# A Mamba, cross-attention and FFN layer on one core: output rows placed by indirect DMAs, norms by pairs, ups in plain fp32

## The chip, the core and the metric

The kernel runs on one core of a Trainium2 chip. The metric is the device time of one execution in microseconds, from the first to the last instruction of the program and what the runtime puts around it. Weights are laid out for the kernel on the host ahead of the launch, and the result is reshaped on the host after it; neither is in the time.

## The reference

The input x is 512 tokens (2 sequences of 256) by 512 features, float32. Three blocks follow each other, each on a layer norm of x, each with its result added to x:

```python
x = x + attn(layernorm(x))              # Mamba-2 block, 128 heads of 64
x = x + matmul(fake_quant(layernorm(x)), fake_quant(ctx))    # 8-bit levels, per sequence
x = x + ffn(layernorm(x))

def ffn(x):                              # 16 heads of 32 features
    t = x[:, perm].reshape(tokens, 16, 32)
    t = gelu(einsum('bhd,hdm->bhm', t, up))       # 32 -> 128, exact gelu
    t = einsum('bhm,hmd->bhd', t, down)           # 128 -> 32
    return t.reshape(tokens, 512)[:, argsort(perm)]

def fake_quant(x, s, z):
    return (clip(round(x / s + z), 0, 255) - z) * s
```

The attention block projects x to 8 groups of 1024 channels with gates and states, takes the RMS norm of each group, and multiplies by an output weight; its last steps are the only ones that the change touches. `perm` is a permutation of the 512 features.

## The kernel before

Everything up to the last group of the attention block (some 740 us of the 809) is a software pipeline over 8 groups of 8 tiles, and the change leaves it alone but for a memset and a small copy. What follows runs once, in straight code, with the order of each engine's instructions written out by hand and semaphores between the engines. Tokens lie in four tiles of 128 (`t`), features in four blocks of 128 (`k`). An fp32 matmul of full precision is made of two or three passes on values split into a high and a low part of type float32r (`h_hi`, `h_lo`), the high part by ScalarE, the low part by VectorE or GpSimd; a matmul on plain float32 takes its operands as they are stored.

1. Attention's end. TensorE multiplies the last three tiles of the group (`out_tile`, 12 matmuls each) and, ahead of the very last one, sums the squares over channels (`last_token_sums`, L1437). VectorE turns the sums to means (L1108), GpSimd raises them to the power -1/2 (L581), and VectorE adds the four token tiles to the residual `res` (L1112). Before that VectorE builds eight 0/1 matrices, `take` and `put` (L999, L1001), which stand for the permutation.
2. Norm for the quantised product. Per pair of token tiles: statistics, power on GpSimd (L640), scale and offset (L1225 to L1227), ScalarE scales (L860), VectorE rounds in two steps (L1232, L1233).
3. Quantised product. TensorE sums the columns of the quantised context `q2` (L1525, one output row), runs 18 matmuls whose result nobody reads (`keep_busy`, WARM_A, L1518), multiplies `negrow` by the column sums with one row of weights (L1533), turns the rounded tiles (L1541), multiplies them (L1549), sums them (L1555), and runs 20 more unread matmuls (WARM_B).
4. Norm for the FFN. VectorE adds the product to `res` (L1268) and normalises all four tiles (L1237); TensorE turns them so that features lie in the partitions (L1566); ScalarE and VectorE split (L876, L1287).
5. FFN. 32 matmuls with `take` permute the features (L1574), and the result is split again (L882, L1291). For each k there are four heads in two pairs: `up_pair` in three passes (L1587), gelu on ScalarE (L885), `down_product` in plain fp32 (L1595).
6. Putting back. VectorE splits the down products (L1296, L1297), 32 matmuls with `put` restore the feature order and turn the result back to tokens by features (`put_back`, L1603), VectorE adds it to `res` (L1301), and SyncE stores four tiles (L502).

## Time and profile before

| what | us |
|---|---|
| median of 3 runs | 809.83 (809.65 to 810.01) |
| the profiled execution's own time | 810.87 |
| its span, first to last instruction | 809.0 |
| mean granted TensorE clock | 0.991 of full |

| engine | busy, share of the span |
|---|---|
| TensorE | 787.9 us, 97% |
| VectorE | 712.9 us, 88% |
| GpSimd | 589.1 us, 73% |
| ScalarE | 548.3 us, 68% |

Busy shares are an average over stages. In the last 68 us, of which this document speaks, the engines hand work to each other, and what matters is which of them ends each wait. Times in a timeline are counted from the start of the span. A matmul in plain fp32 leaves two records in the trace for each one in the program, so that x8 stands for four of them.

### The profile page before, as it was taken

What the parts mean: (1) busy time and instruction counts of PE and PEld (TensorE: products, weight loads), DVE (VectorE), ACT (ScalarE), POOL (GpSimd) and SP (SyncE); (2) the same over time, 40 slices, a digit from 0 to 9 for tenths busy, and PEclk for the clock granted to TensorE, in tenths of its full rate; (3) what the DMA queues carried; (4) which work ended last, traced back from release to release, by engine and by line L of the source; (5) the groups of instructions that cost most, each with busy time, mean ns of one, the idle gap of its engine ahead of it and who ended that gap; (6) DMA issues with size and microseconds to landing.
All of it is one profiled execution on the core that took longest, in us unless ns stands there. A gap on an engine that the chain in (4) does not pass through costs nothing.

```text
span 809.0 us, 14438 instructions
## 1 busy us (share of the span) xinstructions
PE 787.9 (97%) x4244; PEld 615.8 (76%) x4244; DVE 712.9 (88%) x919; ACT 548.3 (68%) x1138; POOL 589.1 (73%) x484
## 2 busy tenths in 40 slices
PE   7989999999999999999999999999999999999987
PEld 6767777777877778777887778877778777777454
DVE  6989999998998989998999989998999989998753
ACT  4777776776676776776667776766667677886242
POOL 5469777887778877797778877788778877785100
PEclk9999999999999999999999999999999999999899
DMA  7453344433443345533454244543444544521001
GB/s 234 154 201 125 125 157 170 157 117 132 169 165 118 119 156 169 169 130 104 168 169 146 101 154 155 169 155 107 144 165 156 166 166 149 184 78 40 1 1 53
DMA packets 44051, 111.14 MB, mean 137 GB/s; under 512 B 5748, under 2 KB 6644, under 8 KB 44020
## 3 DMA queue, kind: packets, MB, share of 16 engines
q1 hardware_dynamic: 44020, 110.76, 40.1%
q8 instruction: 15, 0.25, 0.1%
q14 instruction: 16, 0.13, 0.0%
HBM read 109.30 MB, written 1.44 MB: 137 GB/s over the span
## 4 chain that ended last, share of the span: by engine, by line
PE 93%; DVE 4%; ACT 1%; issue 1%; DMA 1%; POOL 0%; ACTq 0%; SPq 0%; DVEq 0%
PE ps_in L1309 17%; PE ps_in L1311 15%; PE ps_in L1310 15%; PE ps_y L1421 8%; PE ps_o L1309 7%; PE ps_o L1311 7%; PE ps_o L1310 7%; PE ps_y L1424 3%; PE ps_t L1383 3%; PE ps_t L1395 1%; PE ps_o L1603 1%; PE ps_t L1433 1%; PE ps_o L1549 1%; PE ps_o L1587 1%; DVE hid L1010 1%
## 5 line engine op out<-in xcount | busy, mean ns | idle before, releaser
L539 POOL TENSOR_TENSOR w_lo<-raw,w_hi 128x512 fp32r<-128x512 f32 x144 | 233.4, 1642 | 102.9 <-ACT w_hi L647 101.6
L1309 PE MATMUL ps_in<-h_hi,w_hi 128*128 128x512 f32 x560 | 226.3, 404 | 2.8 <-DVE gate L1029 2.8
L1311 PE MATMUL ps_in<-h_hi,w_lo 128*128 128x512 f32 x560 | 219.6, 392 | 0.0
L1310 PE MATMUL ps_in<-h_lo,w_hi 128*128 128x512 f32 x560 | 218.4, 390 | 0.0
L702 ACT ACTIVATE e<-e,nag 128x256 f32<-128x256 f32 (+1 forms) x512 | 183.6, 444 | 2.9 <-DVE nag L1080 2.9
L1010 DVE SCALAR_TENSOR_TENSOR hid<-ps_in,curc,hid 128x510 f32<-128x510 f32 x183 | 136.0, 743 | 4.4
L1309 PEld LDWEIGHTS ps_in<-h_hi,w_hi 128*128 128x128 f32 x560 | 105.1, 188 | 33.2 <-issue 10.5
L1311 PEld LDWEIGHTS ps_in<-h_hi,w_lo 128*128 128x128 f32 x560 | 105.4, 188 | 23.3
L570 POOL TENSOR_TENSOR e<-e,gm 128x512 f32<-128x512 f32 x64 | 100.5, 1570 | 30.8 <-DVE gm L1054 26.8
L1310 PEld LDWEIGHTS ps_in<-h_lo,w_hi 128*128 128x128 f32 x560 | 105.5, 188 | 20.4
L667 ACT ACTIVATE hid<-ps_in,curc 128x512 f32<-128x512 f32 x61 | 47.4, 777 | 102.9 <-PE ps_in L1311 102.7
L1066 DVE TENSOR_TENSOR e<-e,gm 128x1024 f32<-128x1024 f32 x64 | 107.8, 1684 | 2.1 <-DVE curc L1071 1.0
L1309 PE MATMUL ps_o<-wo_hi,z_hi 128*128 128x512 f32 x256 | 101.5, 396 | 0.0
L1311 PE MATMUL ps_o<-wo_hi,z_lo 128*128 128x512 f32 x256 | 99.9, 390 | 0.0
L1310 PE MATMUL ps_o<-wo_lo,z_hi 128*128 128x512 f32 x256 | 99.7, 389 | 0.0
L549 POOL TENSOR_TENSOR wo_lo<-rawo,wo_hi 128x512 fp32r<-128x512 f32 x64 | 85.6, 1337 | 5.3 <-ACT wo_hi L655 5.3
L716 ACT ACTIVATE z_hi<-z,curs 128x512 fp32r<-128x512 f32 x64 | 46.2, 722 | 61.0 <-DVE z L1097 61.0
L1421 PE MATMUL ps_y<-e,hdt 128*64 128x256 f32 x512 | 80.7, 393 | 4.2 <-issue 2.3
L559 POOL TENSOR_SCALAR_AFFINE_SELECT e<-e 128x512 f32<-128x512 f32 x128 | 80.2, 651 | 5.6 <-DMA e<-acs_rows 5.6
L647 ACT ACTIVATE w_hi<-raw 128x512 fp32r<-128x512 f32 x144 | 82.0, 622 | 0.4 <-DMA raw<-in_w_in 0.4
L1097 DVE TENSOR_TENSOR z<-z,gate 128x512 f32<-128x512 f32 x64 | 78.6, 1229 | 2.2
L1037 DVE TENSOR_TENSOR hdt<-ps_t,dtg 128x512 f32<-128x512 f32 x64 | 44.1, 688 | 37.0 <-PE ps_t L1383 34.7
(236 smaller groups left out, 1239.7 us busy)
## 6 DMA issues: line engine op xcount, KB each, us to landing
e<-acs_rows SPq DMA_DIRECT2D x64, 768.0 KB, 4.4
raw<-in_w_in SPq DMA_DIRECT2D x144, 256.0 KB, 4.7
rawo<-in_w_out SPq DMA_DIRECT2D x64, 256.0 KB, 3.7
craw<-in_ctx SPq DMA_DIRECT2D x8, 256.0 KB, 4.1
res<-in_x SPq DMA_DIRECT2D x4, 256.0 KB, 3.6
out_x<-res SPq DMA_DIRECT2D x4, 256.0 KB, 2.2
acs_rows<-z SPq DMA_DIRECT2D x3, 128.0 KB, 2.0
rawo<-in_w_dt SPq DMA_DIRECT2D x1, 256.0 KB, 4.5
```

The source lines that it names most:

```text
L539: pool.tensor_tensor(w_lo[:, slot, :], raw[:, slot, :], w_hi[:, slot, :].bitcast(F32), ALU.subtract).then_inc(s_lo, 1)
L549: pool.tensor_tensor(wo_lo[:, q % WO_RING, :], rawo[:, q % RAWO_RING, :], wo_hi[:, q % WO_RING, :].bitcast(F32), ALU.subtract).then_inc(s_ ...
L559: last = pool.affine_select(out=d, in_=d, compare_op=ALU.is_ge, fill=MASKED, base=0, pattern=[[0, 2], [0, BATCH], [1, P]], channel_multipl ...
L570: pool.tensor_tensor(o, o, gm[:, 1, :, :].rearrange("p b i -> p (b i)").unsqueeze(1) .broadcast_to([P, 2, BATCH * P]), ALU.mult).then_inc( ...
L647: act.activation(w_hi[:, slot, :], raw[:, slot, :], ACT.Copy).then_inc(s_hi, 1)
L702: last = act.activation(a, a, ACT.Exp, bias=nag[:, 2 * b + late, h:h + 1])
L1010: last = dve.scalar_tensor_tensor(y[:, :, a:], src[:, :, 0:SEQ - a], par[:, at + 3 - a:at + 4 - a], y[:, :, a:], ALU.mult, ALU.add)
L1066: dve.tensor_tensor(a, a, g, ALU.mult).then_inc(s_ma, 1)
L1309: pe.matmul(dst, lh, rh, start=first, stop=False)
L1310: pe.matmul(dst, lh, rl, start=False, stop=False)
L1311: return pe.matmul(dst, ll, rh, start=False, stop=last)
L1421: last = pe.matmul(ps_y[rows_, at:at + SEQ], w, e[:, q % E_RING, hh, 0:2, b, :], start=True, stop=False, skip_group_check=True)
```

## The change

- Output order. The matrices `put` and the matmuls with them go. The residual is turned by TensorE to features by tokens (16 transposes, `turn_residual`), kept by ScalarE, stored by SyncE to a scratch tensor in HBM (`x2_dram`) and gathered back by GpSimd with four indirect DMAs, so that its rows lie in permuted order. VectorE adds the down products to these rows, and four more indirect DMAs scatter them to the output, each row to its place. The output leaves the chip as features by tokens and is transposed on the host.
- Norms. Statistics, scales and rounding are ordered tile by tile; the second rounding step and the last normalisation's scaling move from VectorE to ScalarE; the sums of the rounded rows come from ScalarE's accumulator, not from 16 matmuls.
- TensorE. The last output tiles are ordered by token tile, not by channel tile; the sums of squares are split in two; the context's column sums are made with 128 output rows and the rank-one term with 128 rows of weights, of which all but the first are zero; WARM_A goes, and WARM_B goes from 20 to 8.
- FFN. The permuted features are copied, not split, and `up_pair` is one plain fp32 matmul per head on the stored weights and features. Permuting matmuls and ups alternate.

```diff
-WARM_A, WARM_B = 18, 20
+WARM_B = 8
 ...
+            for k in range(DK):                                   # SyncE
+                sp.wait_ge(s_xk, k + 1)
+                sp.dma_start(x2_dram[k * P:(k + 1) * P, :], x2_turned[k]).then_inc(s_xs, 16)
+            sp.wait_ge(s_out, 16 * DK)
 ...
-            pool.wait_ge(s_uph, 1)
-            pool.tensor_tensor(up_lo, up_raw, up_hi.bitcast(F32), ALU.subtract).then_inc(s_upl, 1)
 ...
+            pool.wait_ge(s_xs, 16 * DK)
+            for k in range(DK):
+                pool.indirect_dma_start(x2_rows[k], None, x2_dram[:, :],
+                                        bass.IndirectOffsetOnAxis(ap=perm_col_i[:, k:k + 1], axis=0))\
+                    .then_inc(s_xg, 16)
+            for k in range(DK):
+                pool.wait_ge(s_store, k + 1)
+                pool.indirect_dma_start(out[:, :], bass.IndirectOffsetOnAxis(ap=perm_col_i[:, k:k + 1], axis=0),
+                                        x2_rows[k], None).then_inc(s_out, 16)
 ...
-            z_high_and_square(last_m, CT - 1)
-            act.wait_ge(s_ffw, 32)
-            act.wait_ge(s_in, NIN * GROUPS)
-            act.activation(up_hi, up_raw, ACT.Copy).then_inc(s_uph, 1)
+            square(last_m, CT - 1)
+            z_high(last_m, CT - 1)
 ...
+            def norm_keep(t):
+                act.wait_ge(s_rn, t + 1)
+                act.activation(q1[:, t, :], e1[:, t, :], ACT.Identity, bias=offset[:, :],
+                               accum_out=rowsum[:, t:t + 1]).then_inc(s_q1, 1)
 ...
+            normalise(0)
+            normalise(1)
+            finish_residual(0)
+            finish_residual(1)
+            normalise(2)
+            finish_residual(2)
             act.wait_ge(s_ft, 1)
+            act.activation(f_hi[:, 0, :], feature_bank(0), ACT.Copy).then_inc(s_fhi, 1)
+            act.activation(f_hi[:, 1, :], feature_bank(1), ACT.Copy).then_inc(s_fhi, 1)
+            finish_residual(3)
 ...
+            act.wait_ge(s_xt, 1)
             for k in range(DK):
-                act.wait_ge(s_p, k + 1)
-                act.activation(p_hi[:, k, :], feature_bank(k), ACT.Copy).then_inc(s_phi, 1)
+                act.activation(x2_turned[k], out_bank(k), ACT.Copy).then_inc(s_xk, 1)
 ...
             for k in range(DK):                                   # VectorE
-                dve.wait_ge(s_phi, k + 1)
-                dve.tensor_tensor(p_lo[:, k, :], feature_bank(k), p_hi[:, k, :].bitcast(F32), ALU.subtract)\
-                   .then_inc(s_plo, 1)
+                dve.wait_ge(s_p, k + 1)
+                dve.tensor_copy(e1[:, k, :], feature_bank(k)).then_inc(s_pk2, 1)
+            dve.wait_ge(s_xg, 16 * DK)
             for k in range(DK):
                 dve.wait_ge(s_dn, k + 1)
-                src = feature_bank(k)
-                step_of(dve.tensor_copy(f_hi[:, k, :], src))
-                dve.tensor_tensor(f_lo[:, k, :], src, f_hi[:, k, :].bitcast(F32), ALU.subtract).then_inc(s_dlo, 1)
-            for t in range(TT):
-                dve.wait_ge(s_fin, t + 1)
-                dve.wait_ge(s_late, t + 1)
-                dve.tensor_tensor(res[:, t, :], res[:, t, :], out_bank(t), ALU.add).then_inc(s_store, 1)
+                dve.tensor_tensor(x2_rows[k], x2_rows[k], feature_bank(k), ALU.add).then_inc(s_store, 1)
 ...
-            out_tile(last_m, CT - 2)                              # TensorE
-            last_token_sums()
-            out_tile(last_m, CT - 1)
+            last_token_sums(sqsum)
+            last_out_part(CT - 2, 0)
+            last_out_part(CT - 2, 1)
+            last_token_sums(sq).then_inc(s_ss, 1)
+            last_out_part(CT - 1, 0).then_inc(s_oin, 1)
+            last_out_part(CT - 1, 1).then_inc(s_oin, 1)
+            for t in (2, 3):
+                last = last_out_part(CT - 2, t)
+                last_out_part(CT - 1, t).then_inc(s_oin, 1)
 ...
+            for t in range(TT):
+                rank_one(t)
+            turn_q1(0)
+            turn_q1(1)
+            product(0)
+            product(1)
+            turn_q1(2)
+            turn_q1(3)
+            product(2)
+            product(3)
+            keep_busy(ps_in[:, 0, :], WARM_B)
+            turn_features(0)
+            turn_features(1)
+            pe.wait_ge(s_px, TT)
+            turn_residual(0)
+            turn_residual(1)
+            turn_features(2)
+            turn_features(3).then_inc(s_ft, 1)
+            turn_residual(2)
 ...
-                for w, p in ((up_hi, p_hi), (up_hi, p_lo), (up_lo, p_hi)):
-                    for j in heads:
-                        r = slice(FD * j, FD * (j + 1))
-                        last = pe.matmul(ps_o[:, j, :], w[r, k, :], p[r, k, :], start=(w is up_hi and p is p_hi),
-                                         stop=(w is up_lo), skip_group_check=True)
+                for j in heads:
+                    r = slice(FD * j, FD * (j + 1))
+                    last = pe.matmul(ps_o[:, j, :], up_raw[r, k, :], e1[r, k, :], start=True, stop=True,
+                                     skip_group_check=True)
```

How TensorE's instructions move. In the order of the program, TensorE between the context's sums and the first product, before (`ps_*` are the PSUM banks, `e` holds the rounded tiles, `q` the context):

```order
L1525 MATMUL ps_in<-q,ones_b 1x512 [waits gate_done,taps_done,context_quantised]
L1525 MATMUL ps_in<-q,ones_b 1x512 x7
L1518 MATMUL ps_y<-q,ones_b 128x512 [waits y_free]
L1518 MATMUL ps_y<-q,ones_b 128x512 x17
L1533 MATMUL ps_o<-craw,negrow 128x512 [waits out_added,q2_sums_kept]
L1533 MATMUL ps_o<-craw,negrow 128x512 x3
L1541 MATMUL ps_y<-ident_b,e 128x128 [waits norm_quantised,mean_square_done]
```

The same place now:

```order
L1644 MATMUL ps_in<-q,ones_b 128x512 [waits gate_done,taps_done,context_quantised]
L1644 MATMUL ps_in<-q,ones_b 128x512 x7
L1608 MATMUL ps_o<-craw,zero_point 128x512 [waits q2_sums_kept,out_added,mean_square_done,y_free]
L1608 MATMUL ps_o<-craw,zero_point 128x512 [waits out_added,q2_sums_kept] x3
L1600 MATMUL ps_y<-ident_b,e 128x128 [waits norm_quantised]
```

The 18 unread matmuls are gone, and the rank-one matmuls wait for their own token tile each.

The end of TensorE's program from the second permuting block on, now (L1676 permutes, L1693 is an up, L1701 a down; before, all L1574 stood ahead of all L1587, and the 32 matmuls of L1603 stood last):

```order
L1693 MATMUL ps_o<-e,raw 128x512 [waits permuted_kept,ffn_loaded,residual_turned_kept]
L1693 MATMUL ps_o<-e,raw 128x512
L1693 MATMUL ps_o<-e,raw 128x512 [waits permuted_kept]
L1693 MATMUL ps_o<-e,raw 128x512
L1676 MATMUL ps_y<-h_hi,w_hi 128x512 [waits features_hi,features_lo] x4
L1676 MATMUL ps_y<-h_lo,w_hi 128x512 [waits features_hi,features_lo] x4
L1693 MATMUL ps_o<-e,raw 128x512 [waits gelu_done,permuted_kept]
L1693 MATMUL ps_o<-e,raw 128x512
```

The first ups stand after two permuting blocks of eight matmuls instead of four, and wait also for ScalarE's copies of the turned residual.

The end of GpSimd's program, now; before, it ended with the first of these rows:

```order
L642 TENSOR_TENSOR rstd<-rstd,half 128x2 [waits variance_ready] x4
L653 DMA rawo<-x_rows,perm_col_i 128x512 [waits residual_rows_stored,perm_loaded]
L653 DMA rawo<-x_rows,perm_col_i 128x512
L653 DMA z<-x_rows,perm_col_i 128x512 x2
L658 DMA out_x<-rawo,perm_col_i 512x512 [waits out_rows_ready] x2
L658 DMA out_x<-z,perm_col_i 512x512 [waits out_rows_ready] x2
```

All four gathers wait for all four stores of the turned residual, and the four stores to the output have moved from SyncE's queue to GpSimd's.

## Rows read from the trace of the kernel before

**Rows 1.** The page, chain that ended last, shares of the span by engine:

```profile
PE 93%; DVE 4%; ACT 1%; issue 1%; DMA 1%; POOL 0%; ACTq 0%; SPq 0%; DVEq 0%
```

**Rows 2.** The chain, 747 to 774 us: start us, us, engine, output, line:

```profile
747.12 1.68 PE ps_t L1444 x16
...
751.69 1.82 PE ps_in L1525 x8
753.50 3.99 PE ps_y L1518 x18
757.50 4.13 PE ps_o L1533 x8
761.63 0.98 PE ps_y L1541 x8
...
763.71 5.39 PE ps_o L1549 x16
769.10 0.38 PE ps_y L1555 x16
769.48 4.34 PE ps_in L1518 x20
```

**Rows 3.** The chain, 776 to 803 us:

```profile
776.02 0.61 ACT h_hi L876
...
777.49 4.26 PE ps_in L1574 x16
...
785.37 0.92 PE ps_o L1587 x11
...
795.46 1.07 PE ps_t L1595 x8
796.52 6.14 PE ps_o L1603 x26
```

**Rows 4.** TensorE by stretches: us, busy (instructions), granted clock, DMA share, GB/s:

```profile
757.00:761.00 4.00, 4.00 (x11) 0.94 0.00 0
761.00:767.00 6.00, 5.84 (x25) 0.50 0.00 0
...
773.80:777.40 3.60, 2.17 (x17) 1.00 0.01 2
```

**Rows 5.** VectorE's timeline: start us, us, line, operation, xcount, idle before:

```profile
749.44 0.15 DVE L1108 TENSOR_SCALAR ssum<-ps_t 128x4 f32<-128x4 f32 x1
750.73 1.41 DVE L1112 SCALAR_TENSOR_TENSOR res<-ps_o,rgrp,res 128x512 f32<-128x512 f32 x2 [1.14 <-POOL rgrp L581]
...
772.28 0.69 DVE L1219 BATCH_NORM_STATS2 stats<-res 128x6 f32<-128x512 f32 x1
...
802.69 2.48 DVE L1301 TENSOR_TENSOR res<-res,ps_o 128x512 f32<-128x512 f32 x4 [4.54 <-PE ps_o L1603]
```

**Rows 6.** ScalarE's timeline:

```profile
757.20 1.52 ACT L860 ACTIVATE e<-res,qb,qa 128x512 f32<-128x512 f32 x2 [2.64 <-DVE qb L1227]
...
777.95 2.58 ACT L879 ACTIVATE res<-res,rowq 128x512 f32<-128x512 f32 x4
...
786.31 1.94 ACT L885 ACTIVATE gate<-ps_o 128x1024 f32<-128x1024 f32 x2 [0.30 <-PE ps_o L1587]
```

**Rows 7.** GpSimd's timeline:

```profile
742.51 1.75 POOL L549 TENSOR_TENSOR wo_lo<-rawo,wo_hi 128x512 fp32r<-128x512 f32 x1
749.67 1.02 POOL L581 TENSOR_TENSOR rgrp<-ssum,half 128x4 f32<-128x4 f32 x1 [5.41 <-DVE ssum L1108]
...
754.02 0.70 POOL L640 TENSOR_TENSOR rstd<-rstd,half 128x2 f32<-128x2 f32 x1 [2.06 <-DVE rstd L1216]
```

**Rows 8.** The four stores of the output (durations in ns) and their landing:

```profile
L502 SPq DMA_DIRECT2D out_x<-res x4: 332/335/344, 803.4 to 805.2; - x4
...
DMA to landing us min/median/max: 2.1/2.2/3.4
```

**Rows 9.** SyncE's waits after 800 us: in total, times, longest:

```profile
SPq L157 <- DMA out_x<-res: 3.1, 1, 3.1
```

More of the change, by code:

```diff
@@ L1202, in _, with statistics, add_attention, moments @@
             z_low(last_m, CT - 1)
-            for k in range(DK):
-                one_hot(k)
             mean_square(last_m)
-            def variance(tiles):
+            dve.wait_ge(s_r, GROUPS)
+            def statistics(t):
+                dve.bn_stats(stats[:, t, :], res[:, t, :]).then_inc(s_v, 1)
+                chain[0] += 1
+            def add_attention(t):
+                dve.wait_ge(s_oin, t + 1)
+                add_output(t)
+                dve.wait_ge(s_of, TT * last_m + t + 1)
+                statistics(t)
+            def moments(two):
                 dve.wait_ge(s_v, chain[0])
-                for t in tiles:
+                for t in range(two.start, two.stop):
                     dve.bn_aggr(mv[:, t, :], stats[:, t, :]).then_inc(s_v, 1)
@@ L1214, in variance, with quant_scales @@
                 dve.wait_ge(s_v, chain[0])
[L1215 removed]
                 dve.tensor_scalar(rstd[:, two], mv[:, two, 1], EPS, None, ALU.add).then_inc(s_ev, 1)
[L1218 to L1224 removed]
+            def quant_scales(two):
+                dve.wait_ge(s_ep, 1 + two.start // 2)
                 step_of(dve.tensor_scalar(qa[:, two], rstd[:, two], qd[:, 0:1], None, ALU.mult))
@@ new lines, in add_product @@
+            def add_product(t):
+                dve.wait_ge(s_pr, t + 1)
+                dve.scalar_tensor_tensor(res[:, t, :], out_bank(t), qd[:, 4:5], res[:, t, :],
+                                         ALU.mult, ALU.add).then_inc(s_px, 1)
+                dve.wait_ge(s_px, t + 1)
+                statistics(t)
+            front, back = slice(0, 2), slice(2, 4)
+            add_attention(0)
+            add_attention(1)
+            moments(front)
+            add_attention(2)
+            quant_scales(front)
@@ L1255, in _ @@
+            dve.wait_ge(s_oin, 4)
+            add_output(3)
             round_norm(0)
+            dve.wait_ge(s_of, TT * GROUPS)
+            statistics(3)
             round_norm(1)
-            dve.wait_ge(s_ep, 2)
-            quant_scales((2, 3))
+            moments(back)
+            one_hot(0)
+            quant_scales(back)
+            dve.wait_ge(s_q1t, 1)
+            dve.tensor_copy(q1T[:, 0, 2:4, :], ps_in[:, 0, :].bitcast(BF16).rearrange("p (k n) -> p k n", k=DK)[:, 2:4, :])\
+               .then_inc(s_q1v, 1)
@@ L1283, in _ @@
-            normalise(2)
-            normalise(3)
+            moments(back)
+            one_hot(2)
+            one_hot(3)
+            norm_terms(back)
+            dve.tensor_scalar(e1[:, 3, :], res[:, 3, :], mv[:, 3, 0:1], rstd[:, 3:4],
+                              ALU.subtract, ALU.mult).then_inc(s_fv, 1)
             for k in range(DK):
@@ L1557, in _ @@
-            last.then_inc(s_rs, 1)
-            keep_busy(ps_in[:, 0, :], WARM_B)
-            for t in range(TT):
-                pe.wait_ge(s_f, t + 1)
-                if t == 0:
-                    pe.wait_ge(s_rq, 1)
-                for k in range(DK):
-                    last = pe.transpose(feature_bank(k)[:, t * P:(t + 1) * P], e1[:, t, k * P:(k + 1) * P],
-                                        ident[:, :])
-            last.then_inc(s_ft, 1)
-            pe.wait_ge(s_tp, 2 * DK)
-            for k in range(DK):
-                for d in range(DK):
-                    pe.wait_ge(s_flo, max(k, d) + 1)
-                    for part in (f_hi, f_lo):
-                        last = pe.matmul(feature_bank(k), take[:, d, k * P:(k + 1) * P], part[:, d, :],
-                                         start=(d == 0 and part is f_hi), stop=(d == DK - 1 and part is f_lo),
-                                         skip_group_check=True)
-                last.then_inc(s_p, 1)
+                rank_one(t)
@@ new lines, in _, with take_part @@
+            pe.wait_ge(s_tp, DK)
+            def take_part(k, part):
+                for d in range(DK):
+                    pe.wait_ge(s_flo, max(k, d if part is f_lo else 0) + 1)
+                    pe.wait_ge(s_fhi, d + 1)
+                    last = pe.matmul(feature_bank(k), take[:, d, k * P:(k + 1) * P], part[:, d, :],
+                                     start=(d == 0 and part is f_hi), stop=(d == DK - 1 and part is f_lo),
+                                     skip_group_check=True)
+                return last
```

290 lines of the change are left out of this document (153 added, 137 removed).

## The prediction

> **What bounds the kernel now.** I read the chain of waits first: TensorE holds 93% of the whole span [rows 1], so the kernel is bound by its matmuls as long as the pipeline over the groups runs. The change leaves that part alone up to about 744 us. I then read only the chain after 744 us, to see for each piece whether TensorE worked on something needed, and last the other engines' timelines around it.
>
> Three things stand out. From 753.5 to 761.6 the chain runs through unread matmuls and through a rank-one term with a single row of weights [rows 2]; the work behind them could have gone earlier. From 761 to 767 us the granted clock is 0.50 of full, 1.2 GHz, although TensorE is busy for 5.84 of 6 us [rows 4]: what ran just before was the one-row matmul, and the clock was full until about 760.5 (a mean of 0.94 over 757 to 761 is 0.5 us at half). The 16 product matmuls took 5.39 us partly for that reason [rows 2]. And after the last down product (796.5) 12.5 us go by: 32 matmuls that put the features back, VectorE's add, the store [rows 3, 5, 8]. The ends are 769.1 for the last product, 776.0 for the turned features, 785.4 for the first up, 796.5 for the last down, 809.0 for the span [rows 2, 3].
>
> **Stage A, to the turned features (before: 776.0).** The 16 sums of squares take 1.68 us [rows 2]; half of them now stand one tile earlier, and the square is ahead of the high part on ScalarE. By these durations the sums end at 747.45, VectorE's mean at 747.65 and GpSimd's power, 1.02 us [rows 7], at 748.7; VectorE's first add, at 750.73 before [rows 5], starts at 748.75. TensorE's own work on the attention tiles is the same and ends at 751.65. VectorE's chain is then four adds of 0.70 and four statistics of 0.69 [rows 5] (5.6), two sets of moments and two of scales (0.45 and 0.65 each, estimated from seven steps of about 0.2), and roundings of 0.4; it reaches the second pair's scales at 758.2, with the first pair's tiles rounded by ScalarE at 756.4 and 757.1 (0.76 us for a 128x512, [rows 6]). On TensorE the column sums end at 751.69 + 1.82 = 753.5 [rows 2]. The four rank-one matmuls took 4.13 us, 1.13 of it after 760.5 at half clock, so 3.56 us of work at full clock, 0.89 each; I take the same with 128 rows of weights. They end at 757.1, and the rounded tiles are there: the turns start at 757.1 where before they started at 761.6. The two unread blocks of 3.99 and 4.34 us [rows 2] are the cover of this stage; it is the second one that shrinks to 8 of 20 matmuls, 1.8 us, and what it covered was VectorE's normalisation.
>
> Turns of the first pair 0.6, copies by ScalarE and VectorE 0.65, eight products at full clock 1.8: 760.3. The second pair is scaled from 758.3, rounded on VectorE by 760.3, kept by ScalarE at 760.5 and 761.2, turned by 761.55, copied in two pieces (1.1), multiplied from 762.7 to 764.5: 4.6 us ahead of 769.1. VectorE adds and takes statistics of four tiles from 760.65, 0.7 + 0.7 each with moments, a `take` matrix and short steps between: 767.05 for the last, 772.97 before [rows 5]. GpSimd's power 0.70 [rows 7], the shift, the last tile's norm on VectorE and ScalarE's (0.75 and 0.65, [rows 6]) give 769.75; four turns more, 770.2. Stage A: 776.0 - 770.2 = 5.8 saved. The accumulating form on ScalarE has no row. It costs between nothing and a second pass of 0.75 us; twice on the path, 0 to 1.5; I take 0, by the plain form, and keep the rest for the range.
>
> **Stage B, turned features to the first up (before: 776.02 to 785.37, 9.3 us).** ScalarE's four high parts now have one residual tile between them (0.65, [rows 6]); the low parts end at 773.75. The first high block runs beside that. TensorE needs 0.9 for its low block and 1.8 for the second permuting block (16 matmuls took 4.26 with their first wait, [rows 3]; 0.227 each without). First up at 776.7: 6.5 us, 2.8 saved, because only two of four blocks stand ahead of it. ScalarE's copies of the turned residual, four at 0.5, run from 773.95 to 776.05 beside the second block; this cover is 0.65 us deep.
>
> **Stage C, first up to the last down (before: 11.2 us).** Four heads of ups took 0.92 in three passes [rows 3]. In plain fp32 the nearest row is four heads of downs, 1.07 us [rows 3], so I take 1.05 for four ups. The far bound is that the four do not run side by side: 4 x 0.89 = 3.56. The 12 records in 0.92 us, of which each would need 0.23 alone, speak for side by side. TensorE's work is 4 x 1.05 ups, 2 x 1.82 permuting, 4 x 1.05 downs = 12.05; the wait of the last down for the last gelus (0.97 each, [rows 6]) adds 0.95, handovers 0.3: 13.3 us, 2.1 more than before. Last down at 790.0.
>
> **Stage D, the end (before: 12.5 us).** The last add of 0.70 starts when the last down is done: 790.75. Before, the last store was issued at 805.2, and the span ended at 809.0, 3.8 later: issue 0.33, landing 3.4, the rest the end of the program [rows 8, 9]. Now GpSimd issues; call the time of one indirect DMA on it g. End by this path: 790.75 + g + 3.5. The other path: ScalarE's last copy 776.05, SyncE's store landed at 778.7 (issue 0.33, landing 2.2), four gathers 4g, landing 3.4, the first add 0.7, four scatters 4g, 3.5: 786.3 + 8g. No row shows g. The nearest below is SyncE's issue, 0.33 [rows 8]; above, a whole pass of GpSimd over 128x512, 1.75 [rows 7]. GpSimd takes 0.70 to 1.02 for a handful of numbers [rows 7], and here it has 128 addresses: I take 1.2. The first path gives 795.45, the second 795.9.
>
> **The sum.** 5.8 + 2.8 - 2.1 + (12.5 - 5.4) = 13.6 saved, less 0.5 for the second path, less 1.0: my chain has some 20 handovers at 0.05 us, and this trace has them up to 0.14. That is 12.1: a span of 796.9, an execution of 798.8 by the profiled one's own 810.87. That one lies 1.0 above the median shown, so the prediction is 809.83 - 12.1 = 797.7.
>
> **The Trainium skill against the rows.** Between 773.8 and 777.4 us TensorE did only 16 transposes, busy 2.17 of 3.6 us, and the clock stayed at full, 2.4 GHz [rows 4]. The Trainium skill says the opposite (TensorE: Matmul & The Clock Gate, Part 4: PE-mode transpose): transposes do not count as busy for the clock. By that rule the changed kernel, which has 32 transposes and gaps between 766.3 and 773 and fewer unread matmuls, would drop to half there; this is the second rival. For the stores the Trainium skill (DMA: Bandwidth & Descriptors, Anatomy of one DMA) has about 2.0 us fixed plus the bytes at 436 GB/s for a DMA issued by GpSimd, an estimate of 2.6 for 256 KB; the last store here took 3.4. By the page the end would be 0.8 earlier.
>
> **Rivals.**
> 1. *The clock falls between the products and the permuting blocks.* For it: only transposes and gaps of up to 1.3 us there, and a fall at 760.5. Against: the same mixture in [rows 4] kept it. Price: 16 permuting matmuls (3.65) and the first ups (1.0) at half clock, 4.6 more: 802.3. Chance 0.14.
> 2. *The indirect DMAs cost more on GpSimd than a pass over a tile.* All eight stand in one queue, and the scatters can't start before all gathers have landed. For g above 1.75: 786.3 + 8g + 1.0; at 2.0 a median of 804.1. It ends on the slower side: 809.0 is reached at g = 2.7, and at 3.0 the median is 812. For it: no such instruction in the trace, GpSimd is the slowest engine per element in [rows 7]. Against: the addresses are 128, not 65,536. Chance of g between 1.75 and 2.7: 0.11; above: 0.04.
> 3. *The stage before the turned features saves nothing*, since VectorE and ScalarE, now alternating on single tiles, wait for each other: 797.7 + 5.8 = 803.5. For it: three engines hand over per tile. Against: VectorE's work there gets less. Chance 0.07.
> 4. *The ups don't run side by side*: 4 x 2.5 = 10 more, 807.7. Chance 0.03.
>
> **From the cases to the numbers.** The forecast has 0.61, with 794.8 to 800.5 for itself (g from 0.6 to 1.5, the accumulator up to 1.5, landings 0.8 off). The range goes to 802.8, so that it takes in the first rival and a little of the second, and leaves out under 2 in 10. A change under 0.2%, 1.6 us, can't be told from none here. Slower takes rival 2's end and a trifle for sums of rivals, 0.05; same 0.02; faster 0.93.
>
> **What would show it.** Turns of the rounded tiles start near 757, the last product ends near 764.5, TensorE's clock is full from 757 to 790; the turned features are done near 770 and the first up near 776.7; four ups take 1.05; the last down ends near 790; one indirect DMA holds GpSimd for 1.2 us, and VectorE's first add waits for the first down, not for the gathers. It is wrong if the clock has another 0.50 stretch, if the wait for the gathered rows is the last at VectorE's final adds, or if the time after the last down is far from 5.9 us.

## The result, and the profile after

The changed kernel took 798.05 us (median of 4 runs, 797.97 to 798.31). The kernel before took 809.92 us in the same measurement (4 runs, 809.65 to 811.56). The ratio is 0.9842, with a 95% interval of 0.9821 to 0.9864. The forecast was 797.7, and the time lies in its range. The profiled execution took 798.09 us around a span of 796.3, 12.8 less than the 810.87 around 809.0 of before.

The page of the changed kernel has this chain of the whole span and this new queue (packets, MB, share of 16 engines):

```profile
PE 86%; DVE 7%; issue 2%; ACT 2%; DMA 1%; POOL 1%; SPq 0%; POOLq 0%; DVEq 0%; ACTq 0%
...
q0 software_dynamic: 640, 2.10, 0.8%
```

TensorE has 86% of the chain where it had 93% [rows 1], and the indirect DMAs are there: a queue of their own, 2.10 MB, four gathers and four scatters of 0.26 MB each. Of VectorE's 7%, some 56 us, 16 lie after 744 us, mostly the adds, statistics and rounding of the norms; the others lie in the pipeline ahead. The chain of waits from the first attention add to the turned features (start, us, engine, output, line) passes through VectorE where it passed through TensorE's unread matmuls [rows 2]:

```profile
747.62 1.03 POOL rgrp L584
...
748.67 0.76 DVE res L1175
...
766.38 0.71 DVE stats L1271
...
767.64 0.87 POOL rstd L642
...
770.73 0.03 ACT h_hi L941
```

The first attention add starts at 748.67 (before 750.73, [rows 5]), the last statistics end at 767.09 (before 772.97), and the turned features are there at 770.7 (before 776.0, [rows 3]). TensorE's timeline of the same stretch (start, us, line, operation, output and inputs, count of records, two for each matmul on plain fp32; in brackets the idle time before and what ended it):

```profile
751.60 1.67 PE L1644 MATMUL ps_in<-q,ones_b 128*128 128x512 bf16 x7
753.29 3.67 PE L1608 MATMUL ps_o<-craw,zero_point 128*128 128x512 f32 x8
756.80 0.28 PE L1600 MATMUL ps_y<-ident_b,e 128*128 128x128 bf16 x2
...
758.76 1.89 PE L1616 MATMUL ps_o<-q,e 128*128 128x512 bf16 x8 [1.23 <-DVE e L1331]
...
762.88 1.90 PE L1616 MATMUL ps_o<-q,e 128*128 128x512 bf16 x8 [1.18 <-ACT e L921]
764.62 1.89 PE L1592 MATMUL ps_in<-q,ones_b 128*128 128x512 bf16 x7
```

The rank-one matmuls take 3.67 with 128 rows of weights, the rounded tiles are turned at 756.80, and the 16 products are two groups of 1.9 where they were 5.39 together [rows 2]. Their speed is full because the granted clock is. By stretches (us, busy and instructions, granted clock, DMA share, GB/s) there is no 0.50 left after 745 us [rows 4]:

```profile
757.00:761.00 4.00, 2.77 (x20) 1.00 0.00 0
761.00:764.00 3.00, 1.51 (x10) 1.00 0.00 0
...
770.00:773.00 3.00, 1.84 (x13) 1.00 0.00 0
```

After that TensorE has two permuting blocks, then the ups (L1693) and downs (L1701):

```profile
777.13 1.14 PE L1693 MATMUL ps_o<-e,raw 32*128 32x512 f32 x8
...
784.56 1.07 PE L1701 MATMUL ps_in<-gate,raw 128*32 128x512 f32 x8
...
786.42 1.46 PE L1693 MATMUL ps_o<-e,raw 32*128 32x512 f32 x8
...
790.05 0.60 PE L1701 MATMUL ps_t<-bc,raw 128*32 128x512 f32 x2
```

The last down ends at 790.65. The end of the chain, from the last copy of the turned residual on:

```profile
774.49 2.08 ACT raw L948 x4
776.58 2.92 DMA x_rows<-raw
779.55 0.84 issue
780.39 1.20 POOL rawo L653
...
784.41 3.70 DMA z<-x_rows,perm_col_i
788.13 0.70 DVE rawo L1360
...
789.10 1.00 POOL out_x L658
790.10 0.30 issue
...
792.97 0.97 POOL out_x L658
```

It is the row of eight indirect DMAs that sets the end, not the downs. VectorE's timeline says the same at its final adds (before, it waited 4.54 for the 32 matmuls there, [rows 5]):

```profile
788.13 1.29 DVE L1360 TENSOR_TENSOR rawo<-rawo,ps_in 128x512 f32<-128x512 f32 x2 [3.84 <-DMA z<-x_rows,perm_col_i]
...
790.71 0.69 DVE L1360 TENSOR_TENSOR z<-z,ps_t 128x512 f32<-128x512 f32 x1 [0.70 <-PE ps_t L1701]
```

Down 0 ended at about 785.6, but the first add came at 788.13, when all four gathers had landed. On GpSimd an indirect DMA lasts 0.95 to 1.20, and the next follows 0.30 later, so they stand 1.25 to 1.30 apart, and 1.51 after the first gather. 2.36 us after the last one the span ends; SyncE only waits there, 18.8 us for the scatters, where it waited 3.1 for its own stores [rows 9]:

```profile
SPq L158 <- DMA out_x<-z,perm_col_i: 18.8, 1, 18.8
```

### The profile page after: what moved, and what is told of

Its sections match the earlier page's. It is cut to its first block, busy times and chain, and to the rows that moved or that the text cites. A ratio compares the mean times of both kernels' runs of the same rounds, so it can differ in the third digit from the quotient of the medians.

```text
span 796.3 us, 14339 instructions
## 1 busy us (share of the span) xinstructions
PE 772.0 (97%) x4164; PEld 605.7 (76%) x4166; DVE 704.6 (88%) x901; ACT 553.3 (69%) x1150; POOL 596.7 (75%) x492
## 4 chain that ended last, share of the span: by engine, by line
PE 86%; DVE 7%; issue 2%; ACT 2%; DMA 1%; POOL 1%; SPq 0%; POOLq 0%; DVEq 0%; ACTq 0%
PE ps_in L1368 17%; PE ps_in L1370 15%; PE ps_in L1369 15%; PE ps_y L1480 8%; PE ps_o L1368 7%; PE ps_o L1370 7%; PE ps_o L1369 7%; PE ps_t L1442 3%; PE ps_y L1483 3%; DVE hid L1073 1%; PE ps_t L1454 1%; DVE e L1129 1%; DVE stats L1271 1%; PE ps_t L1492 1%; DMA res<-in_x 1%
## 5 line engine op out<-in xcount | busy, mean ns | idle before, releaser
L686 ACT ACTIVATE hid<-ps_in,curc 128x512 f32<-128x512 f32 x61 | 47.4, 777 | 101.3 <-PE ps_in L1370 101.1
L580 POOL TENSOR_TENSOR sqsum<-sqsum,sq 128x512 f32<-128x512 f32 x55 | 76.2, 1386 | 0.2 <-ACT sq L745 0.2
```

## The experiments

The pipeline ahead of 745 us does not take the same time in each execution: in the profiles of the kernel before and its variants the first attention add starts between 748.4 and 753.1 us, in those of the changed kernel and its variants between 747.5 and 750.7. So beside the medians I compare in each profile the **tail**: from the start of VectorE's first attention add to the end of the span. Before it is 809.0 - 750.73 = 58.3 us, after 796.3 - 748.67 = 47.6, and in a second profile of the unaltered changed kernel 48.0. Tails of the same kernel differ by up to 0.4, so a difference of 0.3 says nothing. Each block of rows has its own run of the kernel before.

| run | median us (lowest to highest) | ratio to before, 95% | tail |
|---|---|---|---|
| one row of weights and sums | 800.41 (799.76 to 801.72) | 0.9881, 0.9858 to 0.9905 | 49.4 |
| gathers from the input | 797.06 (795.66 to 799.58) | 0.9840, 0.9809 to 0.9871 | 46.3 |
| before, plain ups | 810.92 (809.81 to 812.03) | 1.0004, 0.9991 to 1.0016 | 58.3 |
| before, full rows | 808.68 (806.01 to 812.69, and one at 2743.84) | 0.9987, 0.9967 to 1.0007 | 55.9 |
| changed kernel again | 799.85 (798.90 to 800.49) | 0.9875, 0.9856 to 0.9893 | 48.0 |
| semaphore per gather | 796.62 (795.84 to 796.99) | 0.9835, 0.9820 to 0.9850 | 46.4 |
| and downs earlier | 797.18 (796.47 to 797.93) | 0.9848, 0.9833 to 0.9863 | 46.75 |
| plain stores | 796.39 (793.25 to 796.57) | 0.9827, 0.9806 to 0.9848 | 45.2 |
| no unread matmuls | 798.39 (796.63 to 799.56) | 0.9845, 0.9822 to 0.9868 | 47.4 |
| 20 unread matmuls | 800.04 (798.41 to 801.62) | 0.9874, 0.9855 to 0.9893 | 48.75 |
| before, full rows, first unread block out | 810.44 (806.38 to 813.99) | 0.9991, 0.9967 to 1.0015 | 56.0 |
| semaphore per gather, downs spread | 795.83 (795.18 to 797.93) | 0.9821, 0.9799 to 0.9844 | 46.6 |

The kernel before had 810.39 in the first block (rows 1 to 4), 809.99 in the second (5 to 8) and 811.19 in the third. One run of the fourth row took 2743.84, for a reason that nothing here shows; its ratio is without it.

### Was the clock part of the gain?

```diff
-last = pe.matmul(ps_in[:, b, :], ones_b[:, :], q2[:, b * DK + k, :],
+last = pe.matmul(ps_in[0:1, b, :], ones_b[:, 0:1], q2[:, b * DK + k, :],
...
-pe.matmul(out_bank(t), zero_point[:, :], craw[:, t // 2, :], start=True, stop=False,
+pe.matmul(out_bank(t), zero_point[0:1, :], craw[0:1, t // 2, :], start=True, stop=False,
```

> The changed kernel, but the context's column sums are made with one output row and the rank-one term with one row of weights, as before the change. Theory (the one-row matmuls make the clock fall): the trace shows a granted clock of 0.50 for a stretch of 3 us or more between 757 and 767 us, the product matmuls (1.9 us for eight at full clock) take up to twice that, and the median is 1.8 to 3.6 us above the changed kernel's 798.05: 799.8 to 801.6. Rival (the clock fell before because of idle time or of transposes, or by chance): the clock stays at 1.00 and the median stays within 0.3 us of 798.05, since these matmuls have the same number of columns.

In the changed kernel with one-row matmuls the half clock is back, by stretches and at the products:

```profile
757.00:761.00 4.00, 3.31 (x13) 0.55 0.00 0
761.00:764.00 3.00, 3.00 (x14) 0.50 0.00 0
```

```profile
754.17 4.01 PE L1608 MATMUL ps_o<-craw,zero_point 1*128 1x512 f32 x8
...
759.84 3.60 PE L1616 MATMUL ps_o<-q,e 128*128 128x512 bf16 x8 [0.69 <-ACT e L912]
...
765.46 1.90 PE L1616 MATMUL ps_o<-q,e 128*128 128x512 bf16 x8 [1.18 <-ACT e L921]
```

The same eight products took 3.60 at 0.50 and 1.90 at full. The features are turned 23.8 us after the first attention add, against 22.1 in both profiles of the changed kernel, and the tail is 1.4 to 1.8 longer than theirs. The reverse, on the kernel before, changes only these two kinds of matmul (the column sums as above, the other way round):

```diff
-        negrow = sb("negrow", [1, P])
+        negrow = sb("negrow", [P, P])     # zero but for row 0
...
-pe.matmul(out_bank(t), negrow[:, :], colrow[:, t // 2, :], start=True, stop=False,
+pe.matmul(out_bank(t), negrow[:, :], craw[:, t // 2, :], start=True, stop=False,
```

> The kernel before with one part of the change alone: the context's column sums have 128 output rows, and the rank-one term 128 rows of weights, all but the first zero. The 18 and 20 unread matmuls stay. Theory (the one-row matmuls make the clock fall): the clock stays at 1.00 from 757 to 773 us, the four rank-one matmuls take 3.6 instead of 4.13 us, the 16 products 3.7 instead of 5.39, and the median falls by 1.0 to 2.5 us, to 807.4 to 808.9, not by all of the 2.5 since VectorE's four adds and statistics of 1.4 us each then hold the products' end. Rival (idle time does it): the clock falls to 0.50 as before and the median stays at 809.9 within 0.3.

Its clock is 1.00 from 751 to 790, and the 16 products take 3.62 instead of 5.39 [rows 2]. TensorE's timeline of it:

```profile
754.81 3.60 PE L1534 MATMUL ps_o<-craw,negrow 128*128 128x512 f32 x8
...
759.81 0.29 PE L1542 MATMUL ps_t<-ident_b,e 128*128 128x128 bf16 x2 [0.95 <-DVE e L1234]
...
760.84 3.62 PE L1550 MATMUL ps_o<-q,e 128*128 128x512 bf16 x16
```

The tail is 2.4 shorter. 1.7 of it are there when the features are turned (23.6 us after the first attention add, before 25.3), and 0.7 come at the very end, where the last store landed in 2.7 instead of 3.4. Nothing in the edit touches the stores, but the other profile with full rows has 2.8 and the other one with one row 3.5, and no run tells why. The median is 1.7 lower, but the runs scatter, and the interval just includes no change.

How much the clock costs differs from one execution to the next. The run with plain ups, below, leaves this stage as it is in the kernel before, with one row. Its stretches are:

```profile
757.00:761.00 4.00, 4.00 (x13) 1.00 0.00 0
761.00:764.00 3.00, 2.15 (x17) 0.89 0.00 0
764.00:767.00 3.00, 3.00 (x11) 0.54 0.00 0
```

The rank-one matmuls took 3.70 there, all at full clock, and the clock fell at about 763.3, 1.3 us after they had ended. It was at half for about 3.4 us, where the kernel before had it for about 6.8. The 16 products took 4.84, and the features were turned 24.6 us after the first attention add. So the fall came in all three profiles with one-row matmuls, and the 128 rows save 1.0 or 1.7 us by it in the kernel before. Both runs changed the column sums (one output row) together with the rank-one term (one row of weights), so they do not say which of the two does it. In the kernel before the sums were followed by 4 us of unread matmuls at full clock, which speaks for the rank-one term.

### Did the unread matmuls hold the turns?

The prediction said that TensorE's queue held them. This run takes the first block of 18 out of the kernel above.

```diff
-            keep_busy(ps_y[:, :], WARM_A)
```

> The kernel before with full rows in the column sums and the rank-one term, as in the run of that alone, and without the first block of 18 unread matmuls. Theory (my prediction had the turns of the rounded tiles waiting for TensorE; the trace with full rows shows them waiting for VectorE's rounding, which ended 0.5 us ahead of the first product): once the clock holds, the 18 unread matmuls cover an idle stretch and cost nothing: 55.9 us from the first attention add to the end within 0.4, as with full rows alone, and the first product starts at the same distance of 12.5 us from the first attention add. Rival (the step of the prediction as written: TensorE's queue held the turns): it falls by a further 1 us or more. A third outcome, the clock falling to 0.50 in the idle stretch, would show 57 us or more.

The tail is 56.0, against 55.9 with the block, and the products start 12.45 us after the first attention add in both (765.58 and 760.84). So the block cost nothing there. Look at what the first turns of the second pair wait for, in the fence above and here:

```profile
757.80 5.37 PE L1533 MATMUL ps_o<-craw,negrow 128*128 128x512 f32 x8 [1.97 <-DVE res L1113]
...
764.55 0.28 PE L1541 MATMUL ps_t<-ident_b,e 128*128 128x128 bf16 x2 [0.93 <-DVE e L1234]
```

It is VectorE's rounding (L1234) either way. In the kernel before it looks the same: VectorE's last rounding ended at 762.89, and the last turns came at 762.95. Without the block TensorE idled 1.97 us and the clock was 0.61 of full over 757 to 761, the rank-one matmuls took 5.37 for 3.60, and that too was over before the rounding was.

### Do transposes and gaps let the clock fall?

```diff
-WARM_B = 8
+WARM_B = 0        # and 20 in the other run
```

> The changed kernel without its 8 unread matmuls (WARM_B = 0), so that from the last product near 764.6 to the permuting blocks near 772 TensorE does nothing but 28 transposes. Theory (the rows of the kernel before: transposes and short gaps keep the clock): the granted clock stays 1.00 in all of 757 to 790, the turned features are where they were since ScalarE and VectorE set them, and from the first attention add to the end it takes 47.6 to 48.0 us as in the changed kernel. Rival (transposes don't count as activity, as the Trainium skill has it on TensorE: Matmul & The Clock Gate, Part 4): the clock shows 0.50 for 3 us or more somewhere between 766 and 778, and it takes 1.5 to 5 us more.

> The changed kernel with the 20 unread matmuls of before in place of 8 (WARM_B = 20), 2.6 us more of TensorE. Theory (in the changed order these matmuls now stand on the path, since VectorE's norms of the first pair are done at 765.5): the features' turns start at 769.0 instead of 766.4, all features are turned 1.3 to 1.8 us later, and it takes that much longer from the first attention add to the end: 49.0 to 49.6 us. Rival (VectorE and ScalarE set the end of this stage anyway): no difference within 0.3.

Without unread matmuls, TensorE's timeline and its stretches are:

```profile
763.25 1.90 PE L1616 MATMUL ps_o<-q,e 128*128 128x512 bf16 x8 [1.18 <-ACT e L921]
766.77 0.44 PE L1628 MATMUL ps_in<-ident,e 128*128 128x128 f32 x2 [1.61 <-ACT e L902]
```

```profile
764.00:767.00 3.00, 1.39 (x8) 1.00 0.00 0
767.00:770.00 3.00, 2.29 (x17) 1.00 0.00 0
770.00:773.00 3.00, 1.98 (x14) 1.00 0.00 0
```

From 765.15 to 772.5 there are only transposes and gaps, one of 1.61 us, and the clock is 1.00 throughout; the tail is 47.4 to the 47.6 of the changed kernel. This bears on the rule of the Trainium skill (TensorE: Matmul & The Clock Gate, Part 4: PE-mode transpose) that was weighed in the prediction: by it the clock would have fallen, and the trace does not agree, neither here nor at [rows 4]. (That transposes could raise a clock that is at half, no run shows.) With 20 of them TensorE is late: the features are turned 23.1 us after the first attention add instead of 22.1, and the tail is 48.75, 0.75 to 1.15 longer than the two of the changed kernel, a little less than was expected.

### What sets the end?

First the gathers are made free: they read the kernel's input `x`, early, instead of the stored residual, so that the output lacks what the first two blocks added.

```diff
-            pool.wait_ge(s_xs, 16 * DK)
+            pool.wait_ge(s_zlo, STEPS)      # and s_zhi, s_sq
             for k in range(DK):
-                pool.indirect_dma_start(x2_rows[k], None, x2_dram[:, :],
+                pool.indirect_dma_start(x2_rows[k], None, x[:, :],
```

> The changed kernel, but the four gathers read rows of the input x and start once their buffers are free, near 768 us, instead of waiting for the stores of the turned residual; the residual after the second block is left out of the output, x stands in its place. Theory (the end is held by the chain stores, gathers, adds, scatters): VectorE's first final add starts with the first down product near 785.7 instead of 788.1, the last scatter starts at 791.7 instead of 793.0, and the median is 796.9, 1.2 under the changed kernel. Rival (the last down product alone sets the end): the last scatter starts when it did, and the median stays at 798.0 within 0.3.

The adds now wait for the downs, and three of the four scatters for their adds; the tail is 1.3 shorter (1.7 against the second profile):

```profile
786.77 1.48 DVE L1363 TENSOR_TENSOR rawo<-rawo,ps_in 128x512 f32<-128x512 f32 x2 [1.48 <-PE ps_in L1704]
```

```profile
792.69 0.97 POOL L660 DMA_INDIRECT out_x<-z,perm_col_i  x1 [0.80 <-DVE z L1363]
```

The same can be had with the right data, if an add waits for its own gather only:

```diff
-            dve.wait_ge(s_xg, 16 * DK)
             for k in range(DK):
+                dve.wait_ge(s_xg[k], 16)
                 dve.wait_ge(s_dn, k + 1)
```

> The changed kernel, but each of the four gathers has a semaphore of its own, and each of VectorE's final adds waits only for its own gather, where all four waited for all gathers. Theory (the end is held by the chain of gathers and scatters, which waits at the first add for the last gather): the first add starts with the first down product, near 785.7, the last add ends with the last down near 791.4 as before, the last scatter starts at 791.7 instead of 793.0, and from the first attention add to the end it takes 46.3 to 46.5 us instead of 47.6. Rival (the last gather's landing or the last down sets the end whatever the adds wait for): 47.6 within 0.3.

> The changed kernel once more, unaltered, on the chip of the next three, so that differences of about 1 us can be read against it. From VectorE's first add of the attention output to the end of the span it took 47.6 us in the first trace; expected 47.6 within 0.3 again, and a median near 798.

```profile
785.91 0.69 DVE L1360 TENSOR_TENSOR rawo<-rawo,ps_in 128x512 f32<-128x512 f32 x1 [1.48 <-PE ps_in L1701]
```

The first add waits for its down, and the two last scatters for theirs. The tail is 46.4, 1.2 to 1.6 below the two of the changed kernel, and the medians of the same block are 796.62 and 799.85, with no run of the one above the lowest of the other. In the two profiled executions, 3.5 apart, 1.9 lie ahead of the first attention add and are not the edit's. The highest run of this version, 796.99, is also below the lowest of the changed kernel in the first measurement, 797.97.

Then the stores: plain ones from SyncE, which leave each row where it stands in the tile.

```diff
-                pool.wait_ge(s_store, k + 1)
-                pool.indirect_dma_start(out[:, :], ..., x2_rows[k], None).then_inc(s_out, 16)
...
+                sp.wait_ge(s_store, k + 1)
+                sp.dma_start(out[k * P:(k + 1) * P, :], x2_rows[k]).then_inc(s_out, 16)
```

> The changed kernel, but the four final stores are plain ones from SyncE to rows in order, so that the placing of the output rows is left out. Theory (the scatters, 1.26 us apart on GpSimd, are late by their queue): the adds are as in the changed kernel, the last at 791.4; its store is issued at once instead of at 793.0, with 0.33 instead of 0.97 us for the issue, and the landing of a plain store takes up to 1 us longer than the 2.4 from the end of the last scatter to the end of the span: 46.0 to 47.0 us from the first attention add. Rival (a store issued by GpSimd costs what one by SyncE does): 47.6 within 0.3.

The tail is 45.2, 2.4 to 2.8 shorter, more than was expected. The last add ends at 791.0, and the span 2.5 later; with scatters in a row on GpSimd the last add ended at 791.4 and the span 4.9 later. The plain stores landed in 2.0 to 2.2; up to 3.4 had been allowed for.

Two more tried to shorten the version with a semaphore per gather:

```diff
             up_pair(5)
             down_product(0)
-            down_product(1)
             up_pair(6)
             up_pair(7)
+            down_product(1)
             down_product(2)
...                                   # and the last residual tile is turned before d == 2 of the first block
```

> The same semaphores, and two moves on TensorE: the last residual tile is turned between the second and the third high block of the first permuting group, not after the fourth, and the last two pairs of ups stand ahead of the second down product. Theory: the copies of the residual start 0.7 to 1.0 us earlier, and the last down ends 0.7 to 0.9 us earlier, since the last two gelus start that much earlier; with the gathers out of the way the end follows the last down, and from the first attention add to the end it takes 45.4 to 45.8 us. Rival (the last two gelus and their ups are held by the earlier gelus on ScalarE, whatever the order): 46.4 as in the run with the semaphores alone.

```profile
785.57 1.00 POOL L658 DMA_INDIRECT out_x<-rawo,perm_col_i  x1 [2.18 <-DVE rawo L1360]
788.82 0.98 POOL L658 DMA_INDIRECT out_x<-rawo,perm_col_i  x1 [2.24 <-DVE rawo L1360]
...
791.38 0.97 POOL L658 DMA_INDIRECT out_x<-z,perm_col_i  x1 [0.30 <-issue]
```

My theory missed. The last add did come 0.5 earlier (41.6 us after the first attention add instead of 42.1), but down 1 now stood beside the last two, three scatters came due together, and they leave 1.28 apart: the tail was 46.75, not under 46. So I put down 1 between the ups:

```diff
             up_pair(6)
+            down_product(1)
             up_pair(7)
-            down_product(1)
```

> The kernel with the shorter end, but the second down product stands between the last two pairs of ups, so that the last three downs no longer end within 2.6 us of each other. Theory (in that kernel GpSimd's scatters, 1.28 us apart, held the end, three of them queued behind the second add): the second scatter starts 0.8 us earlier, the last scatter starts when the last add is done and not at the end of a queue, and from the first attention add to the end it takes 46.1 to 46.4 us instead of 46.75. Rival (the last down moves back by as much as the queue gains): 46.75 within 0.2 or more.

The second scatter left at 787.47, but the last add moved back to 42.2, and the tail, 46.6, is what the rival said, above the theory's 46.1 to 46.4. On these two orders nothing is gained that these runs can tell; the 795.83 is the lowest median of its block, and its interval overlaps that of the simpler version.

### Are plain fp32 ups worth something alone?

```diff
-for w, p in ((up_hi, p_hi), (up_hi, p_lo), (up_lo, p_hi)):
-    for j in heads:
-        last = pe.matmul(ps_o[:, j, :], w[r, k, :], p[r, k, :], ...)
+for j in heads:
+    last = pe.matmul(ps_o[:, j, :], up_raw[r, k, :], e1[r, k, :], start=True, stop=True, ...)
```

> The kernel before with one part of the change alone: the permuted features are copied by VectorE and the ups run in plain fp32 on stored values (the old kernel's other matmuls as they were). Theory (my stage C: a plain fp32 up costs a little more than three passes, and the split was hidden beside the permuting matmuls): four heads of ups take 1.05 to 1.15 us instead of 0.92, and the median is 0.3 to 0.8 us over 809.9, that is no change that can be measured. Rival (the split on two engines was on the path): ups start earlier, and the median falls by 1 us or more.

The ratio is 1.0004 and the tail 58.3, both as before, but inside the tail two differences cancel. The shorter time at half clock, told above, brought the turned features 0.65 us earlier. From there to the first up it took 9.3 us as before. From the first up to the end of the last down it took 11.9 against 11.2: four ups take 1.14, against 0.92 [rows 3], and where the second pair waits for a gelu the two pairs take 2.04 one after the other. So in the old order plain ups cost about 0.65 us, within the 0.3 to 0.8 of the theory, and the shorter copies gave nothing back.

## Why the prediction was right, and where it was not

**The whole.** By the ends of its stages, the saving of 12.7 us in the span is 5.3 + 2.95 - 2.35 + 6.85; the forecast had 5.8 + 2.8 - 2.1 + 6.6, less 1.0 for handovers. No stage is off by more than 0.5. The 1.0 for handovers stood for no place in particular, and the stages fell short of their sum by only 0.35. That the median came within 0.35 us of the forecast is partly luck. The spans of the two profiled executions differ by 12.7, more than the 12.1 of the forecast, but the profiled execution of the kernel before lay 0.95 above its median and that of the changed kernel at its own, so the medians differ by 11.9. The runs test stage A in part, the ups of stage C and the end of stage D. That fewer permuting blocks stand ahead of the ups (B), and that indirect DMAs replace the 32 matmuls (D), no run tests alone: there the gain is the difference of two traces.

**Stage A: the total right, one step wrong.** The sum for the first attention add (748.75 against 748.67), the last product (764.5 against 764.6, where the next matmuls begin) and the last statistics held. But I had TensorE's queue, with its two unread blocks as the cover, hold the turns of the rounded tiles. Without the first block nothing moved (tails 55.9 and 56.0): the products waited for the turns of the second pair, and those for VectorE's rounding. The gain is 2.1 by the earlier first add, 1.7 by the clock, and the remaining 1.5 by working in pairs and single tiles (the turned features come 25.3 us after the first add before, 23.6 with full rows alone, 22.1 after); this last part is a difference, with no run of its own. Of the 2.1, 1.9 belong to the order: the last matmul of the attention tiles starts 0.57 or 0.58 us after the first add in each profile of the kernel before and its variants, and 2.47 or 2.48 after it in each of the changed kernel and its variants. The clock's 1.7 holds for the profile that the forecast was read from; the runs have 1.0 to 1.7 on the kernel before and 1.8 on the changed one. I had put down the 1.13 us of the rank-one matmuls at half clock and the products as a sum on TensorE, and it came out right since the products' half clock did lie on the path. That 128 rows cost a rank-one matmul no more than one is right: the four took 3.60 to 3.67 with 128 rows, and 3.70 with one at full clock.

The 0.5 that the stage fell short has a place. After the last norm the sum had four turns, 0.45 us. There were eight, since ScalarE's norm of the third tile waits for the same scales as VectorE's of the fourth; they ran from 769.60 until ScalarE took the result at 770.73, 1.13 us:

```profile
769.60 0.44 PE L1628 MATMUL ps_in<-ident,e 128*128 128x128 f32 x2 [0.61 <-ACT e L902]
```

**The accumulating form.** It was open between 0 and 0.75. ScalarE's timeline has it as an instruction of its own:

```profile
755.45 0.71 ACT L891 ACTIVATE e<-e,offset 128x512 bf16<-128x512 f32 x1
756.06 0.19 ACT L891 ACTIVATION_READ_ACCUMULATOR e<-e,offset 128x1 f32 x1
```

0.19 each, and by the profile's chain none of it on the path: the chain goes from ScalarE's scaling (758.33) to VectorE's rounding (759.88) and on through VectorE's adds, past the accumulating instructions. So the 0 that I took is right.

**Stages B and C.** 6.4 us for 6.5, and 13.5 for 13.3. Four plain ups took 1.14 (1.05 was taken, from the downs' row), side by side as taken: a pair by itself, in the run with the downs spread, took 1.13. The far bound of 3.56 was not approached. The last four took 1.46, because their second pair started 0.33 after the first: it waits for the gelu that ended at 786.60.

**Stage D: the right path in the sum, the wrong one in the text.** The path over stores, gathers and scatters was worked out at 795.9 and measured at 796.3. Its terms: copies 0.5 late; landing of the stores 2.9 for 2.65; a wait of 0.84 until GpSimd's first gather, which I had not; four gathers 4.97 for 4.8; their landing 2.77 for 3.4; a handover of 0.27; four scatters 4.84 for 4.8; the end 2.36 for 3.5. So g comes to 1.24 for the gathers and 1.21 for the scatters, for the 1.2 taken between 0.33 and 1.75. The terms that were too low add up to 2.1 and those that were too high to 1.8, so that the sum of this path is right in part by luck. The sentence that VectorE's first add would wait for the first down and not for the gathers contradicts this sum, and it was wrong: it waited 3.84 us for the gathers. One of the prediction's own signs of being wrong, a wait for the gathered rows at the final adds, thus came true. The run with a semaphore per gather shows what that wait costs, 1.2 to 1.6 us. The landing of a scatter that the Trainium skill (DMA: Bandwidth & Descriptors, Anatomy of one DMA) gives by its fixed part and rate, the estimate of 2.6, is near the 2.36 from the last scatter's end on GpSimd to the span's end, and the 2.77 from the last gather's end to VectorE's add; the row of before that I used, 3.4 for the last store, was too long.

**The rivals.** The clock did not fall in this stretch after the change (first rival; the paragraph on the Trainium skill calls it the second), and it does not fall with fewer unread matmuls either. An indirect DMA costs under a pass of GpSimd over a tile, 1.75, so the second did not come. The norm stage saved 5.3 of 5.8, and the ups ran side by side. The chances of what the range leaves out add up to some 0.24, not to under 2 in 10.

## What to carry to other kernels

When the granted clock falls in a stretch where TensorE is busy, look at the shape of what it does: here it fell during or just after matmuls with one row of weights, and the same with 127 rows of zeros, which take no longer, kept it and gave 1.0 to 1.8 us back. Indirect DMAs placed the rows here for less than the products with a permutation (the time behind the last down fell from 12.5 to 5.65 us), but they leave one by one, about 1.28 apart: let each consumer wait for its own, and let them come due evenly. When a sum takes one of two paths for the end, the list of signs must be read off the same path. And two equal tails do not show that an edit does nothing: compare them stage by stage, since the clock can hide what the edit costs.

## What the runs showed of the hardware

- In all three profiles with rank-one matmuls of a single row of weights (3.7 to 4.1 us of them) the granted clock went from full (2.4 GHz) to 0.50 (1.2 GHz): in the kernel before during them, for about 6.8 us [rows 2, 4]; in the changed kernel with one-row sums ahead also during them, for about 6.8; in the run with plain ups 1.3 us after them, for about 3.4. With 128 rows it stayed at 1.00 in this stretch in ten profiles of eleven; the eleventh is the one with the idle time of 1.97 us.
- 28 transposes with gaps up to 1.61 us over 7.4 us kept the clock at 1.00. An idle time of 1.97 us, in the kernel before with full rows and without its first unread block, was followed by 0.61 over 757 to 761 and 0.95 over 761 to 764. What set these two apart, no run looked at.
- An indirect DMA of 128 rows of 2 KB holds GpSimd for 0.94 to 1.20 us, and the next begins 0.30 later, also when nothing is waited for; a plain store holds SyncE for 0.33, before and in the run with plain stores [rows 8]. From the end of the last scatter to the end of the span 2.36 us went by.
- ScalarE's accumulating form is 0.71 for 128x512 and a read of 0.19, which begins 0.10 before the first has ended; the next one began 0.81 and 0.71 after the first.
- Two plain fp32 ups of 32 rows took 1.13 us, and four on four groups of rows 1.14.
